# A redundant group wait is left out ahead of ten of the 64 gathers that GpSimd issues

## The reference, cut to what matters

```
logits = xt @ Wr + br                        # 8 experts
top_vals, top_idx = top_k(logits, 2)
gate = softmax over the two chosen, 0 elsewhere
h = relu(xt @ W1[e] + b1[e])                 # 128 -> 512
y = h @ W2[e] + b2[e]                        # 512 -> 128
out = sum over experts of y * gate
```

## Time and profile before

| | us |
|---|---|
| three runs | 408.42, 411.36, 411.74 |
| their median | 411.36 |
| the profiled execution | 408.86 |
| its span in the trace | 407.1 |

### The profile page before, as it was taken

The page is one execution under the profiler, slowest core; times in us unless marked ns, Lnnn a source line. Parts: engine busy times, 40 slices in busy tenths (PEclk is TensorE's granted clock), DMA queues, the critical chain, the costliest instruction groups (busy, mean ns, idle before and its releaser), DMA issues. The chain is left out here.

```text
span 407.1 us, 8915 instructions
## 1 busy us (share of the span) xinstructions
PE 331.2 (81%) x2366; PEld 295.5 (73%) x2366; DVE 270.2 (66%) x920; ACT 209.7 (52%) x501; POOL 222.4 (55%) x263
## 2 busy tenths in 40 slices
PE   7996999999970688899999999777499999999000
PEld 7885899989970666577777779777489989998000
DVE  4884677656740479687888986898567766665026
ACT  3743566656740355637567583544256666775002
POOL 4016555565666285463756879660655555665712
PEclk9988999999995598899999999668899999999755
DMA  6791111111111500000000000011111111111154
GB/s 162 216 315 45 42 37 42 41 45 42 40 44 49 206 1 2 0 0 2 1 2 3 0 0 2 2 52 53 40 40 39 42 41 40 41 40 40 45 194 134
DMA packets 18674, 22.23 MB, mean 55 GB/s; under 512 B 4114, under 2 KB 13508, under 8 KB 18628
## 3 DMA queue, kind: packets, MB, share of 16 engines
q1 hardware_dynamic: 13092, 11.18, 9.1%
q0 software_dynamic: 4096, 8.40, 6.9%
q10 hardware_dynamic: 1440, 2.11, 1.4%
HBM read 14.33 MB, written 7.34 MB: 53 GB/s over the span
## 5 line engine op out<-in xcount | busy, mean ns | idle before, releaser
L482 POOL DMA_INDIRECT XG<-xn_rows,rows_in x64 | 61.9, 967 | 79.7 <-DMA XG<-xn_rows,rows_in 32.3
L798 PE MATMUL PS<-XT_all,W1B 128*128 x624 | 87.6, 284 | 8.8 <-DVE XT_all L1459 8.7
L798 PEld LDWEIGHTS PS<-XT_all,W1B 128*128 128x128 f32 x624 | 77.7, 196 | 12.3 <-issue 11.1
L494 POOL DMA_INDIRECT y_rows<-YS,rows_out x64 | 64.0, 1000 | 37.1 <-DMA y_rows<-YS,rows_out 27.7
L810 PE MATMUL PS<-H,W2B 128*128 128x128 f32 x624 | 83.3, 277 | 0.0
L1126 ACT ACTIVATE H<-PS,W1B 128x128 f32<-128x128 f32 x156 | 48.9, 364 | 58.0 <-PE PS L798 57.0
L810 PEld LDWEIGHTS PS<-H,W2B 128*128 128x128 f32 x624 | 76.4, 193 | 0.3
L1489 DVE COPY W2B<-W2S 128x513 f32 x78 | 35.3, 452 | 39.0 <-DVE YT_all L1480 35.0
L1116 ACT ACTIVATE W1B<-W1S 128x516 f32 x78 | 49.4, 633 | 21.4 <-DMA W2S<-in_L_ffn_W 7.6
L655 PE MATMUL PS<-ones 128*128 128x128 f32 x236 | 40.8, 350 | 17.2 <-DMA YT_all<-y_rows 16.2
L655 PEld LDWEIGHTS PS<-ones 128*128 128x128 f32 x236 | 39.6, 264 | 18.5 <-DMA YT_all<-y_rows 16.4
(11 more groups left out here) (204 smaller groups left out, 558.4 us busy)
## 6 DMA issues: line engine op xcount, KB each, us to landing
YT_all<-y_rows SPq DMA_DIRECT2D x8, 512.0 KB, 5.6
W1S<-in_L_ffn_W SPq DMA_DIRECT2D x1, 2048.0 KB, 11.1
W2S<-in_L_ffn_W SPq DMA_DIRECT2D x8, 256.0 KB, 8.3
xn_rows<-XN ACTq DMA_DIRECT2D x8, 256.0 KB, 4.3
X<-in_L_attn_x SPq DMA_DIRECT2D x4, 256.0 KB, 4.9
XG<-xn_rows,rows_in POOLq DMA_INDIRECT x64, 2.5
y_rows<-YS,rows_out POOLq DMA_INDIRECT x64, 2.2
out_x<-X SPq DMA_DIRECT2D x4, 256.0 KB, 2.3
```

The lines of the kernel that those rows point to most:

```text
L482: g.indirect_dma_start(out=XG[:, u, :], out_offset=None, in_=xn_dram, in_offset=bass.IndirectOffsetOnAxis(ap=rows_in[:, i:i + 1], axis=0), ...
L494: g.indirect_dma_start(out=y_dram, in_=YS[:, u, :], in_offset=None, out_offset=bass.IndirectOffsetOnAxis(ap=rows_out[:, i:i + 1], axis=0), ...
L798: last = mm(PS[2 + 2 * half + j % 2][:, c * P:(c + 1) * P], W1B[w][:, h * P:(h + 1) * P], XT_all[:, ds(start, P)], start=True, stop=True)
```

## The change

Ahead of a gather from g8 on, the group's wait (line 477) stays at g8, stays for tiles that were single or whose group is odd, and stays for the first tile of an even group; it goes ahead of the second tile of an even group. With `GROUP_OF[i - 8]` even and equal to that of tile i-9 this is g15, g19, g23, g27 and g31, in both layers: ten waits in the program. These ten gathers keep the wait of line 466. Nothing else changes, and no value that is waited for changes.

```
@@ experts(layer), on POOL @@
                 for i in range(DENSE):
                     u = i % XG_RING
-                    if i >= XG_RING:
+                    if i == XG_RING or (i > XG_RING and (GROUP_OF[i - XG_RING] % 2 or GROUP_OF[i - XG_RING] != GROUP_OF[i - XG_RING - 1])):
 
                         pool.wait_ge(s_xt, layer * len(ARRIVALS) + GROUP_OF[i - XG_RING] + 1)
-                    elif i == 0 or i >= FIRST_ROW:
+                    elif i == 0 or FIRST_ROW <= i < XG_RING:
 
                         pool.wait_ge(s_rows, layer + 1)
                     transfer_written()
```

## The result

| | before | after |
|---|---|---|
| median of 20 runs each | 410.88 us | 414.54 us |
| lowest and highest run | 408.42, 414.02 | 410.41, 418.75 |
| the profiled execution, its span | 408.86, 407.1 | 415.10, 413.4 |

The ratio is 1.0072 with a 95% interval of 1.0046 to 1.0099: 0.7% slower, where 1.1% faster was forecast. It is a ratio of fast runs alone, without the five runs of the changed kernel at 417.0 us and more, which are over 1.5% above its fastest. POOL's timeline of the changed kernel comes first. Of layer 0 it has g0, g14, g15, g31, s0, s19, s20, s22, s31; of layer 1, g0, g31 and s31.

What follows compares the result with a forecast made beforehand. The prediction took POOL's own issuing, g0 to s31 in each expert layer, as the bound. Ten dropped waits at 0.45 us give 4.5 us, so 411.36 - 4.5 = 406.9 us, range 403.9 to 409.0.

Steps and rivals of the forecast that it cites:

- POOL is the bound: Both expert layers, g0 to s31: POOL's own issuing bounds them, and everything after waits for s31.
- the chain's detour over ACT in layer 1: Ahead of s20: chain enters POOL through ACT's copy at 372.43; forecast says s20 needed the copy at 359.05 and didn't wait.
- a rival in which PE binds that layer: Layer 1, 340 to 372 us: PE bounds it, so the gain is only 3.4 us, median 408.0; chance 0.08.
- The price of 0.45 us: Ahead of POOL transfers: a second wait, already satisfied, costs 0.45 us, gap 0.75 instead of 0.30.
- The rule weighed: POOL's extra waits: at a dispatch of about 50 ns each, ten cost 0.5 us, lost in noise; forecast rejected it.
- The sum: Ten gathers over both layers: 10 x 0.45 = 4.5 us less, 411.36 to 406.9 us; chance 0.74.
- The stall of g19: g19 had gaps of 1.12 and 1.04 us instead of 0.75; if these go too, the gain is 5.2 us.
- What is late next: Gathers and scatters move up to 2.25 us earlier; scatter margins are 9.4 and 11.3 us, so nothing takes over.
- The fourth rival: Denser gathers meet DVE's W2 copies, 0.25 us each: 18 meetings eat the gain, 48 cost 12 us (418.9); chance 0.05.
- The port rule: DVE's float32 SBUF copies lock GpSimd from shared ports, delaying every gather they meet; trace agreed only for a few, 0.25 us.
- The second rival: Gaps at the ten gathers: 0.45 us belongs to the place, a wait returns only 0.02; time 411.2; chance 0.07.
- the third: POOL's stalls fall elsewhere; one more of the largest size makes the gain 3.1 us, time 408.3; chance 0.06.

Runs made afterwards that it cites:

- set 1: One-chip run set, before 404.95 us: before again 0.9998, changed kernel again 0.9867, 18 waits dropped 0.9791, the five of layer 0 alone 0.9939.
- all pairs: Kernel before without the group wait ahead of every pair's second tile, 9 gathers per layer instead of 5: ratio 0.9791 (set 1), 1.0140 (set 3).
- long filler: Changed kernel with three POOL memsets in place of each dropped wait, gap 0.93 us: 409.77 us against before's 410.45, ratio 0.9978.
- set 3: One-chip run set, before 411.26 us: changed kernel 1.0061, one memset per dropped wait 1.0110, 18 waits dropped 1.0140, both waits ahead of every scatter 1.0181.
- no redundant: Kernel before without all 32 already passed POOL waits in the expert layers: 423.86 us against 406.64 (1.0448), later 391.03 against 405.59 (0.9647).
- set 6: Run set on the chip of set 3, before 405.59 us: only g15's wait dropped per layer 0.9952, all 32 redundant waits dropped 0.9647.

## Why the prediction was wrong, point by point

**POOL is the bound: right in the prompt condition.** There ten waits gave 5.9 us, eighteen 8.9 and thirty-two 14.6, roughly in proportion, and the waits taken out on POOL show in the end time. That also settles the chain's detour over ACT in layer 1: a rival in which PE binds that layer would cap the gain, and nothing capped it.

**The price of 0.45 us: right.** The gaps went from 0.75 to 0.30 in both conditions, and 8.9 / 18 = 0.49 and 14.6 / 32 = 0.46 us are the price per wait. The rule weighed took the about 50 ns of the sequencer's dispatch, from the Trainium skill's page "DMA: Bandwidth & Descriptors", section on the anatomy of one DMA, as the price of a wait, an estimated 0.5 us for ten. The page doesn't say that of a wait, and these numbers refute it.

**The sum: right for a prompt set.** 4.5 us was forecast, 5.2 as the upper bound; the ratio's interval in set 1, 0.9834 to 0.9899 of 404.95 us, is 4.1 to 6.7 us. The two profiles of set 1 show where the excess lies: both layers together are 7.0 us shorter. Of this 5.0 is in the gaps of the gathers, for ten waits and two stalls of 0.3 us less; the rest is in POOL's own part of single transfers and stays unexplained. The stall of g19 did not simply vanish: in layer 0 the changed kernel has it at g20 (1.12 us), and all pairs has one of 1.05 us at its g14.

**What is late next: the step that failed.** "So nothing takes over. Data, values, transfers and their order are the same." Each margin was worked out with releases as prompt as in the profile at hand: ACT's last copies had 9.4 and 11.3 us in hand. In the execution profiled after, the step times of PE and ACT were not the same, since ACT and DVE were released up to 1.9 us late among the gathers and up to 3.8 among the scatters, again and again, and the last copy of layer 0 came 14.1 us later and ended 0.8 us ahead of s31. The margin was consumed, and POOL waited for ACT, 20.9 us in eight gaps that had been 0.30 or 0.76 each. I had not asked whether the spacing of POOL's transfers reaches other engines at all, and one profile of one condition couldn't show it.

**The other side was among the rivals, with the wrong mechanism.** The fourth rival had denser gathers, but made the gathers themselves longer. By the line of all gathers of the changed kernel (duration min/median/max in ns) they are not:

```profile
L482 POOL DMA_INDIRECT XG<-xn_rows,rows_in x64: 942/946/1197, 28.1 to 336.5; - x64
```

That is the row of before but for 5 ns. The port rule weighed beside it, of the Trainium skill's page "SBUF — State Buffer", thus has nothing to explain here. Nor does it show at the meetings: 34 of before's 64 gathers overlap one of DVE's copies of W2 and take 974 ns in the mean, the other 30 take 960; in the changed kernel 30 do, with 964 against 959. The second rival (the gap isn't the wait's) falls with the gap of 0.30, and the third (stalls) is too small: a stall of 1.4 us more was allowed for, against 20.9 us in the eight gaps.

**Why the sign could differ from the profile shown.** The profile of before was prompt, by its landing times and by its starts, none over 0.5 us late. The runs of the comparison were late, by the profile of after and by the level of before: its median of 410.88 us stands against 404.95, 405.68 and 405.59 in the prompt sets and 406.64 to 411.26 in the late ones. The profiled 408.86 doesn't speak against this, as 3.3 us of it are the long stretch between the layers. That before itself loses in a late set, by its scatters at 0.30, is likely and not shown: its one late profile was the fastest of its ten (405.20 us) and lost nothing, but in the long filler's, whose scatters are those of before, they take 51.6 and 52.4 us instead of 48.05 and 49.6. It would be why after loses just 0.7% though its profiled layers are 10.2 us longer than those of the profile shown.

**What stays open.** Shown is that, in the late condition, the late starts go with close transfers and not with the missing wait. Not shown is who holds the release. One thought, argued only: each transfer signals through many small increments. The Trainium skill's page "DMA: Bandwidth & Descriptors" states, in its section on why a DMA increments its semaphore by 16, that on GpSimd's path each of the 16 DMA engines adds one; no run here counts them. Open too is what makes a set prompt or late: it is not the chip and not the kernel, nor the granted clock (the median of the runs of before is 0.899 in set 1 and 0.903 in set 3), and the time or other load of the machine wasn't tried. The recording is a suspect that no run tests: every run on record has a trace's span and clock, so none shows the kernel unrecorded, and the late traces lack about three in ten records of semaphore updates (3492 to 3697 against 4938 to 5005 in the prompt ones). And whether a single close pair is enough was never seen in a late set. None of the kernels that ran in both conditions beats before in both: "no redundant" is the best in one (391.03 us) and the worst in the other (423.86).

## What to carry to other kernels

A wait that is already satisfied costs 0.45 us ahead of an indirect transfer on POOL, and where POOL's issuing is the bound it pays to remove it; but transfers that then follow at 0.30 to 0.38 us can come with late releases of ACT and DVE behind PE, and 0.75 or more did not. Before a margin is called safe, look whether the page has the landing times of both kinds of transfer (in the late profiles one or both are missing) and how far behind PE's end its consumers start, and take the profile of before again, in the same set as the change: a gain of 3.5% and a loss of 4.5% were the same kernel.

## What the runs showed of the hardware

- An engine that waits for PE starts 0.04 us behind the end of its matmuls as a rule, and 1.65 to 3.16 us behind it at the places shown when POOL's transfers follow at 0.30 us in a late set. TensorE's matmuls keep their length (1.06 and 2.07 us).
- A memset of 128 x 128 on POOL takes 0.22 us, and a transfer behind it starts after 0.16 us, less than the 0.30 behind another transfer. Three take 0.78.
- The same chip was late in set 3 and prompt in set 6, and the kernel before moved from 411.26 to 405.59 us with it.
- POOL's part of a gather that overlaps one of DVE's float32 copies from SBUF to SBUF (0.45 us each) is longer by 0.014 us in the mean than that of the other gathers in the profile of before, and by 0.005 us in that of after.
